# Second slice of a gated delta-rule kernel: rows solved by explicit 4x4 inverses, summed by TensorE

## What is computed

```
def step(S, inp):
    qt, kt, vt, at, bt = inp
    Sd = at[..., None, None] * S
    u = vt - jnp.einsum('bhk,bhkv->bhv', kt, Sd)
    Sn = Sd + bt[..., None, None] * kt[..., None] * u[:, :, None, :]
    o = jnp.einsum('bhk,bhkv->bhv', qt, Sn)
    return (Sn, o)
```

## Time and profile before

| what | value |
|---|---|
| median of 3 runs | 502.45 us (500.09 to 503.19) |
| profiled execution | 502.01 us |
| its span in the trace | 499.1 us |
| VectorE busy | 406.4 us, 81% |
| PE busy | 369.8 us, 74% |
| ACT, POOL busy | 278.7 and 277.4 us, 56% |

### The profile page before, as it was taken

The page is one execution under the profiler, slowest core; times in us unless marked ns, Lnnn a source line. Parts: engine busy times, 40 slices in busy tenths (PEclk is TensorE's granted clock), DMA queues, the critical chain, the costliest instruction groups (busy, mean ns, idle before and its releaser), DMA issues.

```text
span 499.1 us, 8388 instructions
## 1 busy us (share of the span) xinstructions
PE 369.8 (74%) x2389; PEld 308.5 (62%) x2389; DVE 406.4 (81%) x1157; ACT 278.7 (56%) x620; POOL 277.4 (56%) x323
## 2 busy tenths in 40 slices
PE   2856670949848799756396876587999998999970
PEld 1312220418347648756395866587989998999970
DVE  4759999999999999999999799965875744458734
ACT  3588965956227525665557546274564566655520
POOL 1167235779999987754848727701222477433340
PEclk9998985978876799977598867799999999999996
DMA  8185889990000000850500000115212114415005
GB/s 223 43 94 102 104 121 148 109 75 2 0 0 0 2 0 2 343 164 0 84 3 1 1 1 29 52 43 101 60 34 88 65 51 112 133 46 138 29 27 173
DMA packets 50204, 34.99 MB, mean 70 GB/s; under 512 B 10992, under 2 KB 46608, under 8 KB 50032
## 3 DMA queue, kind: packets, MB, share of 16 engines
q1 hardware_dynamic: 46576, 28.80, 30.6%
q0 software_dynamic: 3008, 5.40, 3.5%
q10 hardware_dynamic: 576, 0.26, 0.2%
HBM read 15.26 MB, written 10.27 MB: 51 GB/s over the span
## 4 chain that ended last, share of the span: by engine, by line
DVE 49%; PE 31%; issue 9%; POOL 4%; DMA 3%; ACT 2%; ACTq 1%; SPq 1%; POOLq 0%; DVEq 0%
PE bank L726 13%; DVE U L1497 7%; PE bank L741 7%; DVE S L1510 6%; DVE p L1504 6%; DVE p L1491 6%; DVE X L1460 4%; DVE big L1458 3%; PE bank L580 3%; DVE K L1388 2%; POOL placed_y L928 1%; DVE big L1428 1%; PE bank L540 1%; PE bank L656 1%; PE bank L612 1%
## 5 line engine op out<-in xcount | busy, mean ns | idle before, releaser
L580 PE MATMUL bank<-prod_o,ID 128*128 128x128 f32 x512 | 80.7, 323 | 42.8 <-POOL prod_o L288 21.2
L580 PEld LDWEIGHTS bank<-prod_o,ID 128*128 128x128 f32 x512 | 75.3, 233 | 46.6 <-POOL prod_o L288 23.1
L928 POOL DMA_INDIRECT placed_y<-Q,place x46 | 44.1, 958 | 93.6 <-DVE place L1699 38.7
L726 PE MATMUL bank<-Q,p 128*128 128x128 f32 x736 | 94.3, 276 | 2.3 <-ACT p L1253 2.3
L726 PEld LDWEIGHTS bank<-Q,p 128*128 128x128 f32 x736 | 89.1, 192 | 2.6 <-ACT p L1253 2.5
L1070 ACT ACTIVATE p<-S,GAM 128x64 f32<-128x64 f32 x126 | 48.2, 410 | 70.0 <-DVE S L1510 69.5
L281 POOL TENSOR_TENSOR prod_o<-Q,ST 128x1024 f32<-128x1024 f32 x28 | 64.0, 2285 | 35.9 <-PE bank L584 29.6
L1253 ACT ACTIVATE p<-big 128x1024 f32 x46 | 48.5, 1057 | 45.5 <-PE bank L726 39.1
L1510 DVE TENSOR_REDUCE S<-p 128x64 f32<-128x320 f32 x126 | 55.8, 481 | 0.8 <-ACT p L1070 0.8
L1497 DVE TENSOR_REDUCE U<-p 128x32 f32<-128x288 f32 x128 | 52.8, 447 | 0.0
L1491 DVE TENSOR_TENSOR p<-S,bank 128x256 f32<-128x256 f32 x128 | 49.6, 416 | 0.7 <-ACT bank L1065 0.7
(11 more groups left out here) (222 smaller groups left out, 747.5 us busy)
## 6 DMA issues: line engine op xcount, KB each, us to landing
big<-in_L_ffn_w_dram SPq DMA_DIRECT2D x1, 4096.0 KB, 13.1
big<-big SPq DMA_DIRECT2D x16, 192.0 KB, 4.9
Q<-sorted_h SPq DMA_DIRECT2D x46, 64.5 KB, 2.2
sorted_h<-ZERO SPq DMA_DIRECT2D x2, 1472.0 KB, 18.6
X<-in_L_attn_x_dram SPq DMA_DIRECT2D x8, 256.0 KB, 4.6
big<-big SPq DMA_DIRECT2D x16, 128.0 KB, 5.3
K<-placed_y SPq DMA_DIRECT2D x8, 256.0 KB, 3.3
out_dram<-X SPq DMA_DIRECT2D x8, 256.0 KB, 2.4
```

The source lines that it names most:

```text
L580: pe.matmul(ps, ID[:, :], prod_o[:, k % 2, i, :], start=(i == 0), stop=False, skip_group_check=True)
L726: m = pe.matmul(bank[(1, 6)[g % 2] + k][:, c * P:(c + 1) * P], W1E[g % 2][:, f:f + P], XST[:, g % 3, :], start=True, stop=True)
L928: pool.indirect_dma_start(placed_y[g // NF], bass.IndirectOffsetOnAxis(ap=place[:, g:g + 1], axis=0), YS[:, g % YR, :], None).then_inc(sem ...
```

## The change

For slice 1, `substitute` is replaced. `key_products` writes the entries of the triangle into PSUM (`lower`, bank h), with the sign turned, and keeps the three entries next to the diagonal a second time in SBUF. `invert` makes the explicit inverse of the 4x4 matrix in place by six small instructions. `multiply_solved` makes all products of the inverse's entries and the rows of X_ at once (1536, 1024, 512 elements); it reads one operand from PSUM and one from SBUF. The subtractions on VectorE go: `solve` on PE adds, for each row i = 1, 2, 3, the row itself and its i products (2, 3 and 4 matmuls of 512 columns, 18 in both halves), and `solved` on ACT copies each of the six sums back into X_. `prep_done` counts them (4 in place of 2).

`rsqrt` multiplies in another order and, for the keys, keeps its intermediate in PSUM. The products for `sum_queries` and `sum_keys` are laid out with the dimension outermost, so that PE reads neighbouring columns and POOL writes them 320 or 192 elements apart. The places in the chunk order move: everything from AT_SQUARES to AT_SORT is two chunks later, OUT_AT is 0 to 3 chunks later (group 2 one earlier), `weigh_columns` is two groups later.

```diff
     SOLVE = (11, 20)
+    SOLVE_AT = {(2, 1): ((0, 3), (0, 2)), (3, 1): ((0, 1), (1, 3)), (4, 0): ((1, 2), (1, 1))}
+    SOLVED_AT = {19: (0, 3), 20: (0, 2), 25: (0, 1), 26: (1, 3), 28: (1, 2), 29: (1, 1)}
     W_AT = (0, 2)
     Q_AT = (1, 5)
-    QK_AT = (4, 6, 13, 25)
-    AT_ROWS_GA = 6
-    AT_WOG = NCH // 2 - 1
+    QK_AT = (4, 6, 14, 24)
+    AT_ROWS_GA = 8
+    AT_WOG = NCH // 2 + 7
     AT_DIAG = 15
...
     HC = NCH // 2
-    OUT_AT = {0: (11, 11), 1: (15, 15), 2: (19, 19), 3: (23, 23), 4: (25, 25), 5: (27, 28), 6: (30, 31), 7: (33, 34),
-              8: (40, 41), 9: (46, 47), 10: (49, 50), 11: (53, 54), 12: (57, 58), 13: (61, 62)}
-    AT_SQUARES, AT_SUMS, AT_ROOT = HC + 3, HC + 4, HC + 6
-    AT_STATS, AT_ROWS = (HC + 12, HC + 14), HC + 15
+    OUT_AT = {0: (11, 11), 1: (15, 15), 2: (18, 18), 3: (23, 24), 4: (27, 30), 5: (31, 32), 6: (33, 35), 7: (36, 37),
+              8: (41, 42), 9: (48, 49), 10: (51, 52), 11: (55, 56), 12: (58, 59), 13: (61, 62)}
+    AT_SQUARES, AT_SUMS, AT_ROOT = HC + 5, HC + 6, HC + 8
+    AT_STATS, AT_ROWS = (HC + 14, HC + 16), HC + 17
     AT_SHIFT = AT_ROWS + 2
...
+        def by_dimension(region, pairs):
+            return region[:, 0:pairs * HD].rearrange("p (k x) -> p k x", k=HD)
+        def query_terms(j):
+            return by_dimension(QK if j else Q0, SCH * C * (C + 1) // 2)
+        def key_terms():
+            return by_dimension(TMP, SCH * C * (C - 1) // 2)
         def query_products(j):
...
             for d in range(C):
-                size = SCH * (C - d) * HD
-                tiles.append((QK if j else Q0)[:, at:at + size].rearrange("p (n i k) -> p n i k", n=SCH, i=C - d))
+                size = SCH * (C - d)
+                tiles.append(query_terms(j)[:, :, at:at + size].rearrange("p k (n i) -> p n i k", n=SCH))
                 at += size
...
                 size = SCH * (C - d)
-                tiles.append((TMP[:, at * HD:(at + size) * HD].rearrange("p (n i k) -> p n i k", n=SCH, i=C - d),
+                tiles.append((key_terms()[:, :, at:at + size].rearrange("p k (n i) -> p n i k", n=SCH),
                               bank[4][:, at:at + size].rearrange("p (n i) -> p n i", n=SCH)))
...
+        def lower(h):
+            return bank[h][:, 0:9 * SCH].rearrange("p (n e) -> p n e", n=SCH)
+        def lower_entry(h, i, j, count=1):
+            first = (C - 1) * j + i - j - 1
+            return lower(h)[:, :, first:first + (count - 1) * (C - 1) + 1:C - 1]
+        def solved_products(h, j):
+            at = SCH * 2 * HD * sum(C - 1 - i for i in range(j))
+            m = C - 1 - j
+            return big[:, 3072 * h + at:3072 * h + at + SCH * m * 2 * HD].rearrange("p (n i x) -> p n i x", n=SCH, i=m)
+        def solved_row(h, i):
+            return slice_rows(X_[h], 1).rearrange("p (n i) x -> p n i x", i=C)[:, :, i, :]
+        def solved_sum(h, i):
+            b = ((None, 0, 5, 0), (None, 0, 4, 1))[h][i]
+            return bank[b][:, 0:SCH * 2 * HD].rearrange("p (n x) -> p n x", n=SCH)
         def query_rows(j, d):
...
                 pe.wait_ge(sem("qk_ready"), j + 1)
+                if j == NHALF + 1:
+                    pe.wait_ge(sem("prep_done", 0), 3)
                 if j == 0:
...
                 pairs = SCH * C * (C + 1) // 2
-                terms = (QK if j else Q0)[:, 0:pairs * HD].rearrange("p (x k) -> p x k", k=HD)
                 for k in range(HD):
-                    m = pe.matmul(bank[7 if j == 1 else 5][:, 0:pairs], ID[:, :], terms[:, :, k], start=(k == 0), stop=(k == HD - 1))
+                    m = pe.matmul(bank[7 if j == 1 else 5][:, 0:pairs], ID[:, :], query_terms(j)[:, k, :], start=(k == 0), stop=(k == HD - 1))
                 m.then_inc(sem("qk_ps"), 1)
...
                 pairs = SCH * C * (C - 1) // 2
-                terms = TMP[:, 0:pairs * HD].rearrange("p (x k) -> p x k", k=HD)
                 for k in range(HD):
-                    m = pe.matmul(bank[4][:, 0:pairs], ID[:, :], terms[:, :, k], start=(k == 0), stop=(k == HD - 1))
+                    m = pe.matmul(bank[4][:, 0:pairs], ID[:, :], key_terms()[:, k, :], start=(k == 0), stop=(k == HD - 1))
                 m.then_inc(sem("kk_ps"), 1)
+            def solve(h, i):
+                pe.wait_ge(sem("solved_terms"), h + 1)
+                if (h, i) == (0, 2):
+                    pe.wait_ge(sem("qk_evac"), NHALF + 1)
+                elif i == 1:
+                    pe.wait_ge(sem("prep_done", 0), C if h else 2)
+                pe.matmul(solved_sum(h, i), ID[:, :], solved_row(h, i), start=True, stop=False)
+                for j in range(i):
+                    m = pe.matmul(solved_sum(h, i), ID[:, :], solved_products(h, j)[:, :, i - j - 1, :], start=False, stop=(j == i - 1))
+                m.then_inc(sem("solved_ps"), 1)
             def attend(s, q):
...
                     sum_keys(1)
-                if g - 2 == W_AT[1]:
                     sum_queries(NHALF + 1)
...
                     sum_outputs(g, h)
+                    for hh, i in SOLVE_AT.get((g, h), ()):
+                        solve(hh, i)
...
                 for hh in range(NHALF):
-                    pool.wait_ge(sem("prep_done", hh), 1 if hh == h or h == 0 else 2)
+                    pool.wait_ge(sem("prep_done", hh), 1)
+                if h == 1:
+                    pool.wait_ge(sem("kk_ps"), 1)
                 K4 = slice_rows(K_[h], 1).rearrange("p (n i) d -> p n i d", i=C)
...
+            def solved(h, i):
+                act.wait_ge(sem("solved_ps"), (C - 1) * h + C - i)
+                act.activation(solved_row(h, i), solved_sum(h, i), ACT.Copy).then_inc(sem("prep_done", h), 1)
             def evacuate_weights():
...
                     evacuate_weights()
+                if n in SOLVED_AT:
+                    solved(*SOLVED_AT[n])
                 if AT_DIAG <= n < AT_DIAG + B // 2:
...
                 dve.wait_ge(sem("root_out"), count)
-                yield from settle(dve.scalar_tensor_tensor(out=t, in0=half, scalar=-4.0, in1=half, op0=ALU.mult, op1=ALU.mult))
-                yield from settle(dve.scalar_tensor_tensor(out=t, in0=var, scalar=eps, in1=t, op0=ALU.add, op1=ALU.mult))
+                yield from settle(dve.scalar_tensor_tensor(out=t, in0=var, scalar=eps, in1=half, op0=ALU.add, op1=ALU.mult))
+                yield from settle(dve.scalar_tensor_tensor(out=t, in0=t, scalar=-4.0, in1=half, op0=ALU.mult, op1=ALU.mult))
                 dve.scalar_tensor_tensor(out=y, in0=t, scalar=3.0, in1=half, op0=ALU.add, op1=ALU.mult).then_inc(sem("roots_ready"), 1)
...
                 n2, rt, rn, a = bank_vectors(h, s)
-                yield from rsqrt(n2, K_EPS, d2, rn, t_)
+                yield from rsqrt(n2, K_EPS, d2, rn, rt)
                 dve.tensor_tensor(slice_rows(K_[h], s), RAW[h][:, :, 0, :].rearrange("p d t -> p t d"), over(rn), ALU.mult)\
...
                 beta, a, n2, rt, rn, t_, d2, d3 = slice_vectors(h, s)
-                diag = L[:, :, C * d:C * C:C + 1]
+                diag = lower_entry(h, d, 0, C - d) if s else L[:, :, C * d:C * C:C + 1]
                 if s == 0:
...
                 a = bank_vectors(h, s)[3]
-                yield from settle(dve.tensor_tensor(w, at(beta, 1, C) if d == 1 else w, at(a, 1, C + 1 - d), ALU.mult))
+                if s == 1 and d == 1:
+                    yield from settle(dve.scalar_tensor_tensor(out=w, in0=at(beta, 1, C), scalar=-1.0, in1=at(a, 1, C), op0=ALU.mult, op1=ALU.mult))
+                else:
+                    yield from settle(dve.tensor_tensor(w, at(beta, 1, C) if d == 1 else w, at(a, 1, C + 1 - d), ALU.mult))
+                if s == 1 and d == 1:
+                    dve.wait_ge(sem("uw_started", h), 3)
+                    yield from settle(dve.tensor_tensor(at(beta, 1, C), sums, w, ALU.mult))
                 last = dve.tensor_tensor(diag, sums, w, ALU.mult)
...
-            def substitute(h, s, j):
-                X4 = slice_rows(X_[h], s).rearrange("p (n i) d -> p n i d", i=C)
+            def substitute(h, j):
+                X4 = slice_rows(X_[h], 0).rearrange("p (n i) d -> p n i d", i=C)
                 if j == 0:
-                    dve.wait_ge(sem("uw_started", h), 2 * (s + 1))
+                    dve.wait_ge(sem("uw_started", h), 2)
                 m = C - 1 - j
...
                     yield
-                    dve.wait_ge(sem("prep_done", h), s + 1)
+                    dve.wait_ge(sem("prep_done", h), 1)
+            def invert(h):
+                beside = slice_vectors(h, 1)[0]
+                t_ = slice_vectors(h, 1)[5]
+                two = t_[:, 0:2 * SCH].rearrange("p (n e) -> p n e", n=SCH)
+                one = t_[:, 2 * SCH:3 * SCH].unsqueeze(2)
+                other_ = bank_vectors(h, 1)[3][:, 0:SCH].unsqueeze(2)
+                yield from settle(dve.tensor_tensor(two, lower_entry(h, 2, 1, 2), at(beside, 1, C - 1), ALU.mult))
+                yield from settle(dve.tensor_tensor(one, lower_entry(h, 3, 1), at(beside, 1, 2), ALU.mult))
```

(32 more changed lines are left out.)

1 line of the change is left out of this document (removed).

## The result

The changed kernel takes 484.18 us (median of 4 runs, 482.18 to 485.55), the kernel before beside it 502.82 us (500.09 to 504.50). The ratio is 0.9644, with a 95% interval of 0.9605 to 0.9683: 18.6 us less. The forecast was 487.0, in a range of 483 to 495. The profiled execution of the changed kernel has 482.18 us, with a span of 480.4, so 1.8 us lie around the span (2.9 before). It is the fastest of the four executions, so a reading of it alone flatters the change: the profiled pair differs by 19.8 us, the medians by 18.6. Part of the gain lies outside the span: in all 47 executions of the changed kernel and its variants the time holds 1.7 to 1.8 us more than the span, in those of the kernel before 1.8 to 3.0, mostly about 2.5. Why is not known.

The account below looks back on a forecast made before the run. The prediction took VectorE to set the pace while slice 1 is prepared beside the loop, with POOL close behind. VectorE's terms summed to -17.6 us, of which 15.0 reached the end: 502.0 - 15.0 = 487.0 us, range 483 to 495.

Parts of the forecast that it names:

- VectorE's sum: VectorE in the loop, preparing slice 1: all its savings and added instructions together, -17.6 us.
- the subtractions: Slice 1's preparation on VectorE: six subtractions go, -12.1 us, about 5 of it waiting for POOL.
- Products: Slice 1's six products on VectorE: one operand now in PSUM, so no wait for POOL, -2.1 us.
- Roots' steps: Root steps on VectorE with two SBUF operands: 2.99 and 1.83 us fall to 0.28 each, -4.3 us.
- The wait for key sums: VectorE's wait for PE's key sums goes as PE reads neighbouring columns: -0.95 us.
- The small steps: Added on VectorE: one key product and six small instructions per half, about 0.13 us each, +1.8 us.
- The value taken for a repeated PSUM operand: VectorE's products with a small operand repeated 16 times from PSUM: extra cost taken as 0, bounds 0 and +4.4 us.
- PE's 18 matmuls at 0.95 us: Solving matmuls of 512 columns on PE: 0.95 us each, bound 1.9; no loss at 0.95, no slack at 1.9.
- POOL's far writes: POOL's products written far apart: loss 0; rivals: doubling, 500.2 us, chance 0.10; 2.5 times, 512.8 us, chance 0.04.
- The sorted rows are late next, by 3 us: After the loop: sorted rows arrive 3 us after PE is free, so its first expert tile gains 14.6 us.
- nothing late behind the loop: Rival: the expert loop's start-up hides the sort's tail, so the whole 17.6 us is gained: 484.4 us, chance 0.08.
- PE or PSUM dearer: Rival: solving matmuls at 1.9 us lose 3 to 6 us, or PSUM products 4.4; 490 to 493 us, chance 0.18.

Follow-up runs that it names:

- the second execution: The changed kernel run again, unaltered, on a third chip: 485.9 us against 501.0 for the kernel before, ratio 0.968; its profiled execution took 486.2 us.

## Why the prediction was right

**VectorE's sum: -17.6 forecast, -17.7 measured.** Term by term: the subtractions are gone (-12.1 by the forecast; no run has this term alone). Products 7.3 us, spacing as forecast. Roots' steps 0.3 us. The wait for key sums is gone. The old root costs 4.1 in the changed kernel (forecast 4.3), the old layout 1.8 (forecast 0.95). The small steps stay at 0.2 us. Taken from the kernel before, the root alone didn't give its term, root and layout together did. In the whole change the terms add up, and it leaves VectorE no instruction with two SBUF operands in that stretch for POOL to hold up.

**The value taken for a repeated PSUM operand, 0 between 0 and +4.4, was right:** 1.22 us for 1024 elements, as with both operands in SBUF and POOL silent. By that, the rule cited from Advanced Engine Details and Errata (Trainium skill, on PSUM cachelines) has no price for this VectorE read, an operand of which each entry is repeated 16 times.

**PE's 18 matmuls at 0.95 us: 17.1 forecast, 17.7 measured.** The upper bound of 1.9 us was a true bound for columns far apart (33.2 us for 18). The query sums, forecast at 4.7 us, took 4.5 in the second half and 7.3 in the first, where the granted clock was low; there was room for it. POOL's far writes cost nothing (6.05 against 6.03 us). The rule cited from the GPSIMD Engine Reference (Trainium skill, on pitfalls of Q7 kernels) speaks of reads; here the far read has 31% (2.57 against 1.96 us) and the write nothing.

**After the loop: the term that was mis-sized.** "The sorted rows are late next, by 3 us": measured 0.22 in one execution and 1.68 in another. The forecast let the scatters come 17.6 - 5.6 = 12.0 us earlier. Their last is 14.6 earlier (308.36), and the read back 15.5. Three things make the difference. The loop started 1.0 us earlier, which had been put at 0 (0.7 of it was there ahead of the changed code, so it belongs to the execution; in the other runs of the changed kernel and its variants the first state is at 82.4 to 83.8 us). The scatters hang on the sort only by way of PE's ranks, PE's outputs of group 12 and POOL's group 13, and there about 1.6 us went. The most of it is a wait of VectorE for PE's logits ahead of the ranks, in the row below, which is of the kernel before; VectorE has no such wait now, and PE's four turns ahead of it take 0.66 us where they took 1.12. And SyncE started 2.3 us behind the last scatter, not 3.2. The first tile therefore gained 18.4 us and not 14.6, the end 18.7 and not 15.0. Another 1.1 us came from around the span, which the prediction held at 2.9. Against these 4.8 us, the profiled execution lies 2.0 below the median, and so the forecast of 487.0 is 2.8 us above the 484.2 measured. The time came near the rival *nothing late behind the loop* (484.4), though its mechanism is not shown: in the second execution the rows are late, and that one has 486.2 us, close to the forecast. That the first one lies so near 484.4 is luck.

```profile
287.13 0.29 DVE L1542 TENSOR_TENSOR RT<-bank,RB 128x128 f32<-128x128 f32 x1 [1.17 <-PE bank L656]
```

**What the two chunks later cost** is at most these 0.2 to 1.7 us ahead of the first tile, and they are lost again in the loop where slice 0's work is put earlier. That the new places alone make the kernel before 3.3 us slower was measured only among stalls that the forecast did not know.

**The rival *PE or PSUM dearer*** had one place too few. Its mechanism exists, and at 1.9 us a matmul it would have cost 11.1 us of the loop, not 3 to 6.

## What to carry to other kernels

Where the same instruction has two durations in a timeline, find out what the long ones have in common (here two SBUF operands while POOL works) before pricing an edit: taking away one of them can leave most of its gain in other waits (0.7 of 4.3 us here), taking away all of them gained the sum, and a tiny operand placed in PSUM was worth 7.3 us, as much as the subtractions' own work. When an edit adds work to a second engine, look at every result that stands behind it on that engine, not only at its own due time. Ahead of a "late next" term, follow the chain to the thing that is late instruction by instruction: the chunk number that it is scheduled at need not be what releases it.
